# Second causal window's operands loaded behind the first's; two chunks normalised on ScalarE and their low parts made on GpSimd

## What is computed

```python
x = x + attn_a(layernorm(x))      # 16 heads of 8, softmax over all keys
x = x + ffn(layernorm(x))         # down(silu(gate(x)) * up(x)), hidden 384
x = x + attn_b(layernorm(x))      # the same with a causal mask
x = x + ffn(layernorm(x))

def _layernorm(x, axis=-1, eps=1e-05):
    m = jnp.mean(x, axis=axis, keepdims=True)
    v = jnp.var(x, axis=axis, keepdims=True)
    return (x - m) / jnp.sqrt(v + eps)
```

## Time and profile before

| | us |
|---|---|
| device time, median of 3 runs | 1323.11 (1322.62 to 1324.69) |
| the profiled execution: device time | 1321.39 |
| its span, first to last instruction | 1319.5 |
| PE busy / DVE busy / ACT busy / POOL busy in it | 1270.7 / 1162.8 / 1002.3 / 142.6 |

### The profile page before, as it was taken

The page is one execution under the profiler, slowest core; times in us unless marked ns, Lnnn a source line. Parts: engine busy times, 40 slices in busy tenths (PEclk is TensorE's granted clock), DMA queues, the critical chain, the costliest instruction groups (busy, mean ns, idle before and its releaser), DMA issues.

```text
span 1319.5 us, 26665 instructions
## 1 busy us (share of the span) xinstructions
PE 1270.7 (96%) x9681; PEld 648.6 (49%) x9681; DVE 1162.8 (88%) x2979; ACT 1002.3 (76%) x1791; POOL 142.6 (11%) x309
## 2 busy tenths in 40 slices
PE   8899999999999999999997998899999999999898
PEld 6444343434343434343434875455555555555487
DVE  7689999999999999999934988699999999999376
ACT  8678888888888888888885552477877777777743
POOL 5630000000000000000001210200000000000011
PEclk9689999999999999999998997699999999999999
DMA  7611011111011111001000242212211221130001
GB/s 212 206 33 34 16 20 34 34 34 34 18 17 34 34 33 34 22 14 34 2 2 0 81 128 86 60 35 51 51 35 34 55 47 35 37 64 2 3 25 40
DMA packets 40059, 58.43 MB, mean 44 GB/s; under 512 B 7796, under 2 KB 19448, under 8 KB 39928
## 3 DMA queue, kind: packets, MB, share of 16 engines
q1 hardware_dynamic: 39928, 56.72, 18.0%
HBM read 36.77 MB, written 18.87 MB: 42 GB/s over the span
## 4 chain that ended last, share of the span: by engine, by line
PE 88%; DVE 5%; ACT 3%; issue 2%; DMA 1%; POOL 1%; SPq 0%; DVEq 0%; POOLq 0%
PE psum L1178 30%; PE psum L1110 21%; PE psum L1144 20%; PE psum L1265 4%; PE psum L1036 3%; PE psum L1249 2%; PE psum L1152 2%; ACT probs L656 2%; DVE maxima L888 1%; PE psum L1047 1%; DVE hid L966 1%; PE psum L1194 1%; PE psum L1085 1%; PE psum L1021 1%; PE psum L1162 1%
## 5 line engine op out<-in xcount | busy, mean ns | idle before, releaser
L656 ACT ACTIVATE probs<-psum 128x512 f32<-128x512 f32 (+3 forms) x1386 | 822.1, 669 | 174.2 <-PE psum L1144 89.5
L888 DVE TENSOR_REDUCE maxima<-psum 128x1 f32<-128x512 f32 x1232 | 767.8, 680 | 27.0 <-PE psum L1110 23.9
L1144 PE MATMUL psum<-qop,kop 64*128 64x512 f32 (+3 forms) x1792 | 513.7, 422 | 9.1 <-ACT probs L656 7.5
L1110 PE MATMUL psum<-kop,qop 62*128 62x512 f32 (+2 forms) x1744 | 499.7, 426 | 9.8 <-DMA kop<-k_parts 5.5
L1178 PE MATMUL psum<-probs,v 128*32 128x512 f32 (+3 forms) x3584 | 436.6, 563 | 1.1 <-ACT sums L663 1.1
L1144 PEld LDWEIGHTS psum<-qop,kop 64*128 64x128 f32 x1792 | 255.4, 188 | 213.4 <-ACT probs L656 186.2
L1110 PEld LDWEIGHTS psum<-kop,qop 62*128 62x128 f32 x1744 | 252.4, 189 | 214.8 <-DVE maxima L884 93.7
L884 DVE CUSTOM_DVE_ANT_0 junk<-psum,mask 128x384 bf16<-128x384 f32 (+3 forms) x512 | 222.3, 485 | 20.5 <-PE psum L1110 20.1
L1178 PEld LDWEIGHTS psum<-probs,v 128*32 128x32 f32 x3584 | 72.4, 109 | 112.8 <-issue 83.4
L1152 PE MATMUL psum<-half_ident,key_mask 64*128 64x64 bf16 x1024 | 83.2, 197 | 0.0
L539 POOL TENSOR_TENSOR shift<-negmax,zeros 128x16 bf16<-128x16 f32 x64 | 14.1, 220 | 567.6 <-DVE negmax L896 557.4
(11 more groups left out here) (102 smaller groups left out, 732.2 us busy)
## 6 DMA issues: line engine op xcount, KB each, us to landing
qop<-q_parts SPq DMA_DIRECT2D x256, 64.0 KB
kop<-k_parts SPq DMA_DIRECT2D x64, 128.0 KB
kop<-k_parts SPq DMA_DIRECT2D x128, 64.0 KB
q_parts<-parts SPq DMA_DIRECT2D x24, 256.0 KB, 2.9
k_parts<-parts SPq DMA_DIRECT2D x24, 256.0 KB, 3.0
x<-in_L_attn_a_x SPq DMA_DIRECT2D x8, 256.0 KB, 4.2
q_parts<-att SPq DMA_DIRECT2D x8, 256.0 KB, 3.6
k_parts<-att SPq DMA_DIRECT2D x8, 256.0 KB, 3.8
```

Of the source, the lines that this page charges most:

```text
L656: nc.scalar.activation(probs[:, slot, heads[0] % 2:heads[-1] % 2 + 1, c0:], psum[:, bank:bank + len(heads), c0:], ACT.Exp, scale=SCORE_SCA ...
L888: ins = nc.vector.tensor_reduce(dst, src, AX_X, ALU.max)
L1110: ins = mm(psum[:, bank, column:column + width], qop[rows, buf, f, r, qb * P:(qb + 1) * P].bitcast(F32R), kop[rows, buf, r, kh * CHUNK:kh ...
L1144: ins = mm(psum[:, bank + k, c0:], kop[rows, buf, c // 2, j * P:(j + 1) * P].bitcast(F32R), qop[rows, buf, f, c // 2, c0:].bitcast(F32R), ...
```

## The change

Three edits, all in that passage:

- SP: in the second layer `load_operands(1, 1)` stands right behind `load_operands(0, 0)`, ahead of the stores of chunks 3 to 7. In the first layer it stays where it was. The wait for the stores of chunks 6 and 7 stays in both.
- Chunks 6 and 7 of the second attention's layer norm: ACT makes `xn` (`normalise_tail`, four ACTIVATEs with a scale and a bias for each row) in place of DVE (`normalise`, four TENSOR_SCALARs). POOL makes the bias, minus mean times inverse deviation (`negative_centre`, two small instructions behind the inverse deviation).
- Chunks 6 and 7 of its second parts: POOL makes them (`low_parts`) in place of DVE (`split_parts`).

```diff
+TAIL_CHUNK = CHUNKS - 2
...
                 load_operands(0, 0)
+                if layer == 1:
+                    load_operands(1, 1)
                 store_parts(layer, 1, 1)
...
                 if layer == 0:
                     sp.wait_ge(key_rows, 2)
                     sp.wait_ge(query_rows, 2)
-                load_operands(1, 1)
+                    load_operands(1, 1)
...
+            def negative_centre(n, mo):
+                pool.wait_ge(rstd_ready[0], n + 1)
+                nc.gpsimd.tensor_tensor(centre[:, n % 2], mo[:, 0], mo[:, 1], ALU.mult).then_inc(centre_begun, 1)
+                pool.wait_ge(centre_begun, n - TAIL_CHUNK + 1)
+                nc.gpsimd.tensor_scalar(centre[:, n % 2], centre[:, n % 2], -1.0, None, ALU.mult).then_inc(centre_ready, 1)
+            def low_parts(n):
+                pool.wait_ge(part2_ready, CHUNKS + n)
+                pool.wait_ge(part1_ready, CHUNKS + n + 1)
+                dst = parts[:, n % 2]
+                nc.gpsimd.tensor_tensor(dst[:, 1], qk[:, n % 2], dst[:, 0], ALU.subtract).then_inc(part2_ready, 1)
...
                         inverse_deviation(0, moments[:, residual % 2], residual + 1)
+                        if residual >= TAIL_CHUNK:
+                            negative_centre(residual, moments[:, residual % 2])
+                    if qkv_rows is not None and qkv_rows >= TAIL_CHUNK:
+                        low_parts(qkv_rows)
...
+                def normalise_tail(n):
+                    act.wait_ge(centre_ready, n - TAIL_CHUNK + 1)
+                    act.wait_ge(xt_psum[0], n + CHUNKS - 1)
+                    for t in range(TPC):
+                        ins = nc.scalar.activation(xn[:, n % 2, t, :], x[:, n * TPC + t, :], ACT.Identity,
+                                                   scale=moments[:, n % 2, 1, t:t + 1], bias=centre[:, n % 2, t:t + 1])
+                    ins.then_inc(xn_ready[0], 1)
...
                     if turned is not None:
                         copy_ot(turned, 0)
+                    if residual is not None and layer == 0 and residual >= TAIL_CHUNK:
+                        normalise_tail(residual)
                     if ffn is not None:
                         silu(layer * CHUNKS + ffn, 2)
...
-                    if residual is not None and layer == 0:
+                    if residual is not None and layer == 0 and residual < TAIL_CHUNK:
                         dve.wait_ge(rstd_ready[0], residual + 1)
                         normalise(0, residual, moments[:, residual % 2], 0, xn[:, residual % 2], residual + CHUNKS - 1)
                     if qkv_rows is not None:
                         if last_qkv:
                             causal_jobs(*((12, 15) if m == CHUNKS - 1 else (18, 22)))
-                        split_parts(1, qkv_rows, qkv_rows % 2)
+                        if qkv_rows < TAIL_CHUNK:
+                            split_parts(1, qkv_rows, qkv_rows % 2)
```

More of the change, by code:

```diff
@@ L200, in transformer_pair_kernel @@
         power = sb("power", [P, TPC], F32)
+        centre = sb("centre", [P, 2, TPC], F32)
         xn = sb("xn", [P, 2, TPC, E], F32)
@@ L264, in transformer_pair_kernel @@
         first_steps = sem("first_steps")
+        centre_begun = sem("centre_begun")
+        centre_ready = sem("centre_ready")
         first_scale_ready = sem("first_scale_ready")
```

## The result

The changed kernel took 1309.98 us (median of 4 runs, 1308.85 to 1311.29) against 1322.86 for the kernel before on the same chip (1322.61 to 1324.69): a ratio of 0.9903, 95% interval 0.9888 to 0.9918. The forecast was 1315.5 with a range from 1311.5 to 1318.7; the direction was right, and the gain, 12.9 us, was larger than the range allowed. In two later comparisons the same kernel took 1312.15 and 1311.93, ratios 0.9922 and 0.9911, which are gains of 9.6 and 11.3 us. So a fair size of the gain is 10 to 13 us where 7.6 was forecast, and the first comparison stands at its upper end. The profiled execution took 1309.93, its span 1308.1.

What follows compares the result with a forecast made beforehand. The prediction took DVE's work, and behind it the load of window 1, to delay the second layer's first scores; 5.3 + 1.14 + 1.15 = 7.6 us off the median 1323.11 gave 1315.5, range 1311.5 to 1318.7.

Steps and rivals of the forecast that it cites:

- The wait for `kop`: Ahead of the second layer's first scores: loading window 1 early removes PE's 5.54 us wait and gains 5.3 us.
- Chunk 7's second part: On DVE ahead of the last jobs: moving it to POOL takes 1.14 us off the path.
- The jobs between and the ring: Jobs 12 to 17 ahead of chunk 7's products: DVE reaches them earlier, PE waits less for the ring, gaining 1.15 us.
- ACT's four operations: Normalising one chunk on ACT: four ACTIVATEs take at most 1.76 us, with 1.7 as the value used.
- What is late next: POOL's subtraction, last stores, then maxima on SP: operands ready at 823.15, ahead of the scores at 824.8 by 1.65 us.
- The products near 808.7: PE's products of chunk 7 were to start at 808.65 in place of 809.81.
- The normalising of chunk 7: Moved to ACT: `xn` ready when it was before, with PE's transposes staying at 807.24.
- the step on the normalisings: Chunks 6 and 7 moved from DVE to ACT: together taken as zero, from -0.6 to +0.5 us.
- the allowance: Half a microsecond for the clock's phase, put on top of the bounds of the summed gain.
- An own range of 1314.5 to 1317.5: The forecast case's range of end times, for a gain of 8.6 to 5.6 us; chance 0.62.
- the bound of 5.8: Lower bound of the summed gain, in us: normalisings at -0.6 and the 1.15 falling away; upper bound 8.1.
- The clock rival: Behind the first scores: full clock returns with the gap gone, gaining 7.6 + 2 to 4.9 us, about 1312; chance 0.15.

Runs made afterwards that it cites:

- e7_gap_fill: Kernel before with 12 useless matmuls in PE's wait for window 1's operands ahead of the second layer's first scores: 1321.09 us, ratio 0.9990.
- e2_tail: All of the change except the moved load of window 1, against the kernel before: 1315.35 us, ratio 0.9951.
- e16_fill4: Kernel before with four useless matmuls in PE's idle time ahead of the first causal jobs: 1321.13 us, ratio 0.9998.
- e5_load_fill4: Kernel before with only the load of window 1 moved, plus four useless matmuls ahead of the first causal jobs: 1315.20 us, ratio 0.9954.
- e12_norm6: Kernel before with only the normalising of chunk 6 moved to ACT: 1318.86 us, ratio 0.9983.
- e13_norm67: Kernel before with only the normalisings of chunks 6 and 7 moved to ACT: 1317.55 us, ratio 0.9974.
- after: First profiled execution of the changed kernel, with all three edits against the kernel before: 1309.93 us.
- e6_after_fill: Changed kernel with one useless matmul ahead of each of the 20 jobs preceding the second layer's first scores: 1321.11 us, ratio 0.9994.

## Why the prediction fell short

**Right.** The wait for `kop`: 5.50 in the table against 5.3, and the load alone is worth 6.3 at the end. Chunk 7's second part: 1.14 against 1.14. The jobs between and the ring: 1.17 against 1.15. ACT's four operations: 1.65 against 1.7. What is late next, the chain through POOL, the stores and the maxima, with a slack of 1.65: measured 2.3. The products near 808.7 came at 806.60, since all ahead of them was earlier. The normalising of chunk 7: PE's transposes start 5.99 behind the residual addition of chunk 7 in both traces (807.24 less 801.25, 805.20 less 799.21), so moving it did them neither good nor harm.

**Wrong: the step on the normalisings.** "These two together I take as zero, from -0.6 to +0.5." Alone they are worth 3.4 us (1.7 to 5.2). The working weighed DVE's order against ACT's, half a microsecond each way, and took the lengths of PE's work from the trace of before as fixed. They weren't: 6.8 us of that stretch stood at 0.50. Its timeline had the hints: 1.06 us of idle PE ahead of the first causal jobs, then the low clock, then `down` for 2.93 us where at full clock it took 1.60. In this kernel DVE's normalising of chunk 6 is what made PE idle there; taking it off DVE closed that idle time, and the low clock was gone in 11 of 11 profiled executions. Putting the work back on DVE brought both back (one execution). So of the 2.76 in the trace 0.74 is DVE's order, where 0.5 was forecast, and 2.02 the clock, at which the prediction put nothing. The zero came out of 0.5 against 0.6, and neither cancelled the other: the 0.6 is that of chunk 7, and it didn't come, for `xn` was ready 5.90 behind the addition of chunk 7 on ACT and 5.88 on DVE.

**Wrong as well: the allowance.** "Half a microsecond for the clock's phase" is too little. The same changed kernel, in three profiled executions, had 8.3, 14.3 and 13.9 us of low clock behind the first scores, and its 13 runs span 1308.85 to 1315.00, with mean clocks from 0.977 down to 0.972. An own range of 1314.5 to 1317.5 is narrower than that spread. It is also added up wrongly: the bound of 5.8 less half a microsecond is 5.3, not 5.6. And the range's end of 1311.5 cuts off the clock rival's own best case, 7.6 and 4.9, which is 1310.6. In the first comparison all four runs had a mean clock of 0.977, which was luck, since of the nine later runs three had it; the gains of the two later ones, 9.6 and 11.3 us, would have been inside the range of 4.4 to 11.6.

**The clock rival**, at 0.15 and about 1312, forecast the right time for the wrong reason. It wanted the clock back because the 5.5-us gap was gone. But e7_gap_fill fills the gap and gains nothing that can be measured, and e2_tail keeps a gap of 6.04 and gains 6.5 us (0.9951). The low clock that did go away stood 37 us ahead of the scores, behind an idle time of 1 us, which the prediction didn't look at because it isn't the longest.

**The rule of the Trainium skill** that was set beside that rival ("TensorE: Matmul & The Clock Gate", section Why this matters for your kernels: no idle gaps between bursts) is about gaps longer than 1.06 us, and so about the 5.5-us one. In e7_gap_fill the trace agrees as far as the clock rose once that gap was filled; in time it gave nothing that can be measured. Of the short gap the rule says nothing.

**Still open.** A filled gap at 795 (e16_fill4, e5_load_fill4) shows no gain at the end, while the moved normalisings are worth 3.4. The two intervals, 2.4 gained to 1.9 lost and 1.7 to 5.2 gained, still overlap, so it isn't settled that 1 us less idling by itself is worth less. One difference is seen: with chunk 7 on ACT the low clock at 807 lasts 3.4 us in all nine profiled executions without a fill, and with chunk 7 on DVE 6.8 us in seven of eight, before being the eighth. So the moved normalising of chunk 7 may keep what that of chunk 6 wins, but the times of e12_norm6 and e13_norm67 don't tell it, and why the clock falls for longer was not shown. Nor was it shown why the clock held in e7_gap_fill behind the same idle time. Nor was it shown why before's profiled load landed in 3.90 us, while in five executions with the load at its old place it took 5.09 to 5.67; the term of 5.3 may be on the low side by that. The 6.3 us of the load alone fit that. What sets the low clock behind the scores was not found.

## What to carry to other kernels

Before costing an edit with durations from a trace, read the granted clock of each stretch it touches, and ask of every idle time of PE ahead of a low stretch, however short, whether the edit closes it: here the edit that closed 1 us of idling also took away a low clock that had cost 2.0 us on the chain. But count only what an undo and a repeat confirm, since one and the same program has a low spell in one execution and not in the next, and filling idle time bought nothing measurable at one place and some 1.5 us on the path at another. When work goes to GpSimd, look at what VectorE does in that very stretch: a move that gains beside one neighbour gains nothing beside another.

## What the runs showed of the hardware

- Four f32 128x128 TENSOR_SCALARs from SBUF to SBUF took 3.27 us beside a subtraction of 2.34 us on GpSimd, and 1.11 without it. The first of VectorE's four took 2.50 us, where the median of that line is 0.34. The Trainium skill says, in "SBUF — State Buffer", section SBUF: two separate sides, that GpSimd and VectorE, when VectorE works in a mode with two ports or reads two SBUF inputs, share a pair of ports, and that whichever starts first holds it for its whole instruction. The trace agrees in the length, since the long one ends within 0.1 us of GpSimd's (809.54 and 809.46), but not in the order: by the records VectorE's started first, at 807.04 against 807.12, and it was the one that waited. In which mode it worked no run shows. VectorE's reductions from PSUM and its masks beside the same subtraction (after, 803.70 and 811.66) weren't longer: 0.68 and 0.69 us as elsewhere.
- GpSimd's subtraction of 128x1024 f32 took 2.35 us, 1.9 times VectorE's 1.22; the same difference with fp32r output took 2.78.
- The granted clock fell from 1.00 to 0.50 behind a stretch in which PE showed as busy 4.00 of 4.00 us (e6_after_fill), and rose from 0.50 to 1.00 during 5.30 us of back-to-back useless matmuls (e7_gap_fill).
